# Transformer with a mixture of experts: expert inner activations computed feature-major, routing weights laid over partitions through DRAM

## The reference

```python
x = x + attn_part                                   # four layers
xf = layernorm(x).reshape(S, 128)                   # S = 8192 tokens
shared_out = silu(xf @ shared_gate_w.T) * (xf @ shared_up_w.T) @ shared_down_w.T   # 256 inner features
scores = sigmoid(xf @ router_w.T)                   # 16 experts; 4 groups of 4
# the best 2 groups by their two best biased scores, the best 4 experts in them, weights w normed to 1
g = einsum('sc,ech->esh', xf, gate_w); u = einsum('sc,ech->esh', xf, up_w)         # 32 inner features each
hw = silu(g) * u * combine.T[:, :, None]            # combine: w, or 0 where not chosen
x = x + shared_out + einsum('esh,ehc->sc', hw, down_w)
```

## Time and profile before

| what | value |
|---|---|
| median of 3 runs | 2311.6 us (2310.13 to 2312.68) |
| the profiled execution's own time | 2312.34 us |
| its span, first to last instruction | 2310.4 us |
| mean granted TensorE clock | 0.991 of full speed |
| busy over the span | PE 96%, PEld 82%, DVE 82%, ACT 80%, POOL 53% |
| block of experts | from about 1997 us to the end |
| 2080 to 2280 us: busy of 200 us | PE 200.0, PEld 160.8, DVE 152.3, ACT 118.2, POOL 75.0 |

### The profile page before, as it was taken

One profiled execution on the slowest core, in us unless ns is written; L12 is line 12 of the kernel. 1 busy time (PEld: TensorE's weight loads), 2 busy tenths in 40 slices (PEclk: granted clock), 3 DMA queues, 4 the chain that ended last, 5 costly groups with the idle time before them and its releaser, 6 DMA issues. The chain is left out here.

```text
span 2310.4 us, 81563 instructions
## 1 busy us (share of the span) xinstructions
PE 2206.6 (96%) x30592; PEld 1900.8 (82%) x30592; DVE 1894.9 (82%) x4687; ACT 1846.8 (80%) x2741; POOL 1233.4 (53%) x2217
## 2 busy tenths in 40 slices
PE   4899999999999999999999999999999999799998
PEld 3788888888888888888888888888888888688887
DVE  6788888888888888888888888888878886577774
ACT  3688888888888888888888888888878888656554
POOL 4555666655655555556555556565555554333332
PEclk8999999999999999999999999999999999999999
DMA  5444443433344343344434434433444342111100
GB/s 136 125 123 131 124 113 107 111 107 110 109 112 117 107 111 107 108 111 111 111 109 112 111 108 110 112 108 106 113 120 113 107 111 82 31 29 29 28 24 19
DMA packets 268388, 229.55 MB, mean 99 GB/s; under 512 B 37216, under 2 KB 266720, under 8 KB 268000
## 3 DMA queue, kind: packets, MB, share of 16 engines
q1 hardware_dynamic: 268000, 224.32, 35.2%
HBM read 14.46 MB, written 4.19 MB: 8 GB/s over the span
## 5 line engine op out<-in xcount | busy, mean ns | idle before, releaser
L985 DVE TENSOR_REDUCE rowmax<-bank 128x4 f32<-128x1024 f32 (+1 forms) x768 | 908.9, 1215 | 90.1 <-PE bank L582 87.7
L802 ACT ACTIVATE probs<-bank 128x1024 f32<-128x1024 f32 x768 | 737.6, 1024 | 124.0 <-PE bank L641 112.8
L641 PE MATMUL bank<-qstack,kstack 64*128 64x128 f32 (+1 forms) x4096 | 424.5, 300 | 14.7 <-DMA qstack<-maxrows 14.7
L582 PE MATMUL bank<-kstack,qstack 62*128 62x256 f32 (+1 forms) x4096 | 416.7, 301 | 6.5 <-DMA qstack<-base_turned 6.5
L641 PEld LDWEIGHTS bank<-qstack,kstack 64*128 64x128 f32 x4096 | 316.7, 192 | 17.2 <-DMA qstack<-maxrows 17.2
L582 PEld LDWEIGHTS bank<-kstack,qstack 62*128 62x128 f32 x4096 | 316.1, 193 | 6.9 <-issue 6.9
L1148 POOL CAST xn1T_parts<-xn1T 128x256 fp32r<-128x256 f32 x128 | 50.9, 397 | 460.1 <-ACT xn1T L810 460.1
L714 PE MATMUL bank<-w,hidden 128*128 128x128 f32 x2048 | 285.4, 283 | 3.3 <-ACT hidden L850 2.8
L604 PE MATMUL bank<-maskT_half,pick_half 64*128 64x128 bf16 (+1 forms) x3072 | 269.6, 241 | 15.2 <-ACT probs L802 5.4
L661 PE MATMUL bank<-probs,v_pad 128*32 128x256 f32 x4096 | 271.0, 382 | 0.6 <-DVE v_tok L966 0.6
L544 PE MATMUL bank<-mask_half,pick_half 64*128 64x128 bf16 (+1 forms) x3072 | 268.3, 242 | 2.1 <-DVE rowmax L985 0.9
(11 more groups left out here) (149 smaller groups left out, 5099.5 us busy)
## 6 DMA issues: line engine op xcount, KB each, us to landing
qstack<-base SPq DMA_DIRECT2D x384, 128.0 KB, 2.5
kstack<-base SPq DMA_DIRECT2D x384, 128.0 KB, 2.6
qstack<-base_turned SPq DMA_DIRECT2D x384, 128.0 KB, 2.4
turn_x<-turn_c SPq DMA_DIRECT2D x512, 32.0 KB, 1.8
ctx_den<-ctxT_raw SPq DMA_DIRECT2D x256, 64.0 KB, 2.0
ctx_num<-ctxT_raw SPq DMA_DIRECT2D x256, 64.0 KB, 2.0
qstack<-maxrows SPq DMA_DIRECT2D x256, 16.0 KB
out<-ot SPq DMA_DIRECT2D x16, 256.0 KB, 2.4
```

The costliest lines, as they stand in the source:

```text
L582: last = pe.matmul(bank[:, b0 + b, i * wide:(i + 1) * wide], qstack[rows, r, p0 + i, t * 128:(t + 1) * 128], kstack[rows, r, p0 + i, 0:wid ...
L641: last = pe.matmul(bank[:, b0 + b, i * wide:(i + 1) * wide], kstack[rows, r, p0 + i, kt * 128:(kt + 1) * 128], qstack[rows, r, p0 + i, q0: ...
L802: act.activation(probs[:, k], bank[:, A_BANK[k]:A_BANK[k] + 2, :], ACT.Exp, scale=SCALE).then_inc(exp_done[k], 1)
L985: dve.tensor_reduce(rowmax[:, n % 2, t, :, p0:p0 + heads], bank[:, M_BANK[k]:M_BANK[k] + 2, :].rearrange("p b (h c) -> p b h c", h=heads), ...
```

## The change

Only the block of experts is changed (and two constants are added, which moves its lines and those of the layers by two). The stationary operand is now a block of 128 inner features of the weights, and the four tiles of a group, 512 tokens, move past it: for each of FE = 6 feature blocks f one gate product and one up product of 512 columns (`product(q, f)`), whose result is [128 features x 512 tokens], one PSUM bank each. That is the layout the down product wants: `h_turn`, the copies to `hT` and their semaphores are gone, and `down` reads `hw` directly. ACT's silu and DVE's gating now run once per feature block (6 of 512 elements per partition, where 4 of 768 were).

The routing weight now has to vary over the partitions by expert and over the free axis by token. `combine` is transposed on TensorE (`combine_turn`, one matmul per group), copied out by ACT (`rows_out`), stored by SP as 16 rows of 512 numbers in DRAM (`rows_kept`), and read back by four DMAs, each of which repeats four of those rows on 32 partitions (`spread`), together 1 MB into the single buffer `factors`. POOL then multiplies four blocks of [128 x 512] in place (`weighted`), with a full second operand. The normalisation (`norm`) moves from DVE to POOL. The down product of a group runs one group later, two banks hold its results, and the store of a group is split in two DMAs.

```diff
+FE, FR = GU // 128, E * EH // 128
+DOWN_ORDER = tuple(range(FR, FE)) + tuple(range(FR))
...
-        combine = sb("combine", [128, 2, GT, E])
-        gate_act = sb("gate_act", [128, 2, GU])
-        act_all = sb("act_all", [128, 2, GU])
-        hw = sb("hw", [128, 2, E * EH])
-        hT = sb("hT", [128, GU // 128, 128])
+        combine = sb("combine", [128, E, GT])
+        rows = sb("rows", [E * GT, 2, 128])
+        factors = sb("factors", [128, FR, GT * 128])
+        gate_act = sb("gate_act", [128, 2, GT * 128])
+        hw = sb("hw", [128, 2, FE, GT * 128])
         ot = sb("ot", [128, 2, GT, D])
+        rows_kept = nc.dram_tensor("rows_kept", (2, E, GT * 128), F32, kind="Internal").ap()
...
+            def spread(q):
+
+                sp.wait_ge(rows_ready, q + 1)
+                at_least(sp, factors_landed, 16 * SPREAD * (q - 1))
+                sp.dma_start(rows_kept[q % 2].rearrange("e (t n) -> (e t) n", t=GT), rows[:, q % 2]
+                             ).then_inc(rows_stored, 16)
+                sp.wait_ge(rows_stored, 16 * (q + 1))
+                at_least(sp, hw_ready, FR * q)
+                for e in range(SPREAD):
+                    sp.dma_start(factors[e * EH:(e + 1) * EH],
+                                 rows_kept[q % 2].rearrange("(f e) n -> e f n", e=SPREAD)[e:e + 1]
+                                 .broadcast_to([EH, FR, GT * 128])).then_inc(factors_landed, 16)
...
+            for q in SLOTS:
                 if live(q):
+                    spread(q)
+                if live(q + 3):
+                    load(q + 3)
+                if live(q - 2):
+                    store(q - 2)
...
-            def product(n, v, u, i):
-
-                if i == 0:
-                    at_least(pe, act_ready, n - 1)
-                if n == 0 and i == 0:
+            def product(q, f):
+
+                n = FE * q + f
+                if n == 0:
                     pe.wait_ge(weights_split, 2)
-                if u == 0 and i == 0:
-                    pe.wait_ge(xT_low, n // GT + 1)
-                last = product_of_parts(pe, bank[:, 3 * (u % 2) + i, :],
-                                        [xT_parts[:, v % 2, p, u] for p in range(2)],
-                                        [w_in_parts[:, p, i * 512:(i + 1) * 512] for p in range(2)])
-                if i == 2:
-                    last.then_inc(in_done, 1)
-
-            def h_turn(n, u, half):
-
-                if half == 0:
-                    pe.wait_ge(hw_ready, n + 1)
-                    at_least(pe, hT_ready, 2 * n)
-                else:
-                    pe.wait_ge(hT_ready, 2 * n + 1)
-                for i in range(3):
-                    c = 3 * half + i
-                    src = hw[:, u % 2, c * 128:(c + 1) * 128] if c < E * EH // 128 else \
-                        act_all[:, u % 2, c * 128:(c + 1) * 128]
-                    last = pe.transpose(bank[:, 7, i * 128:(i + 1) * 128], src, eye[:])
-                last.then_inc(h_turned, 1)
-
-            def down(n):
-                pe.wait_ge(hT_ready, 2 * (n + 1))
+                if f == 0:
+                    pe.wait_ge(xT_low, q + 1)
+                x = [xT_parts[:, q % 2, p].rearrange("p t c -> p (t c)") for p in range(2)]
+                at_least(pe, gate_ready, n - GATE_BANKS + 1)
+                product_of_parts(pe, bank[:, GATE_BANK + n % GATE_BANKS, :],
+                                 [w_in_parts[:, p, f * 128:(f + 1) * 128] for p in range(2)], x).then_inc(gate_done, 1)
+                at_least(pe, act_ready, n - UP_BANKS + 1)
+                product_of_parts(pe, bank[:, UP_BANK + n % UP_BANKS, :],
+                                 [w_in_parts[:, p, GU + f * 128:GU + (f + 1) * 128] for p in range(2)], x
+                                 ).then_inc(in_done, 1)
+
+            def combine_turn(q):
+                pe.wait_ge(combine_ready, q + 1)
+                pe.wait_ge(xT_ready, min(q + 2, NG))
+                pe.wait_ge(score_ready, q + 1)
+                pe.transpose(bank[0:E * GT, TURN_BANK, 0:128], combine[:].rearrange("p e t -> p (e t)"),
+                             eye[:]).then_inc(combine_turned, 1)
+
+            def down(q, t):
+                n = GT * q + t
+                if t == 0:
+                    pe.wait_ge(act_ready, FE * (q + 1))
                 if n == 0:
                     pe.wait_ge(weights_landed, 16)
-                at_least(pe, out_ready, n)
-                pe.wait_ge(xT_ready, min((n + 2) // GT + 2, NG))
-                pe.wait_ge(score_ready, min((n + 1) // GT + 2, NG))
-                for c in range(GU // 128):
-                    last = pe.matmul(bank[:, 6, 0:D], hT[:, c], w_down[:, c], start=(c == 0),
-                                     stop=(c == GU // 128 - 1))
+                at_least(pe, out_ready, n - 1)
+                for i, c in enumerate(DOWN_ORDER):
+                    if t == 0 and c < FR:
+                        pe.wait_ge(hw_ready, FR * q + c + 1)
+                    last = pe.matmul(bank[:, OUT_BANK + n % OUT_BANKS, 0:D], hw[:, q % 2, c, t * 128:(t + 1) * 128],
+                                     w_down[:, c], start=(i == 0), stop=(i == FE - 1))
                 last.then_inc(down_done, 1)
...
+            for q in SLOTS:
+                if live(q + 1):
+                    x_turn(q + 1)
+                if live(q):
+                    product(q, 0)
+                if live(q):
+                    combine_turn(q)
+                if live(q - 1):
+                    down(q - 1, 0)
+                if live(q + 1):
+                    router(q + 1)
+                if live(q):
+                    product(q, 1)
+                if live(q):
+                    product(q, 2)
+                if live(q - 1):
+                    down(q - 1, 1)
+                if live(q):
+                    product(q, 3)
+                if live(q - 1):
+                    down(q - 1, 2)
+                if live(q):
+                    product(q, 4)
+                if live(q):
+                    product(q, 5)
+                if live(q - 1):
+                    down(q - 1, 3)
...
+            for q in SLOTS:
+                if live(q + 1):
+                    xT_out(q + 1)
+                if live(q):
+                    gate(q, 0)
+                if live(q):
+                    rows_out(q)
+                if live(q + 1):
+                    scores(q + 1)
+                for f in range(1, FE):
+                    if live(q):
+                        gate(q, f)
...
+            def gating(q, f):
+
+                n = FE * q + f
+                at_least(dve, down_done, GT * (q - 1))
                 dve.wait_ge(gate_ready, n + 1)
-                dve.tensor_tensor(act_all[:, u % 2], g[:, GU:2 * GU], gate_act[:, u % 2], ALU.mult
+                dve.wait_ge(in_done, n + 1)
+                dve.tensor_tensor(hw[:, q % 2, f], bank[:, UP_BANK + n % UP_BANKS, :], gate_act[:, n % 2], ALU.mult
                                   ).then_inc(act_ready, 1)
...
+            for q in SLOTS:
+                if live(q - 2):
+                    result(q - 2, 3)
+                if live(q + 2) and q + 2 > 1:
+                    residual(q + 2)
+                if live(q):
+                    gating(q, 0)
+                if live(q + 1):
+                    routing_groups_1(q + 1)
+                if live(q - 1):
+                    result(q - 1, 0)
+                if live(q):
+                    gating(q, 1)
+                if live(q):
+                    gating(q, 2)
+                if live(q + 1):
+                    routing_groups_2(q + 1)
+                if live(q - 1):
+                    result(q - 1, 1)
+                if live(q):
+                    gating(q, 3)
+                if live(q + 1):
+                    routing_experts(q + 1)
+                if live(q - 1):
+                    result(q - 1, 2)
+                if live(q):
+                    gating(q, 4)
+                if live(q + 1):
+                    weights_of_experts(q + 1)
+                if live(q):
+                    gating(q, 5)
...
+            def power(q):
+                pool.wait_ge(mv_ready, q + 1)
+                pool.tensor_scalar(ve[:], mv[:, :, 1], 1e-5, None, ALU.add).then_inc(ve_ready, 1)
+                pool.wait_ge(ve_ready, q + 1)
+                pool.tensor_tensor(rstd[:], ve[:], expo[:], ALU.pow).then_inc(rstd_ready, 1)
+
+            def norm(q):
+                pool.wait_ge(rstd_ready, q + 1)
+                pool.wait_ge(xn_turned, q)
+                for t in range(GT):
+                    last = pool.tensor_scalar(xn[:, t], h_groups[:, q, t], mv[:, t, 0:1], rstd[:, t:t + 1],
+                                              ALU.subtract, ALU.mult)
+                last.then_inc(xn_ready, 1)
+
+            def weighted(q, f):
+
+                pool.wait_ge(factors_landed, 16 * SPREAD * (q + 1))
+                pool.wait_ge(act_ready, FE * q + f + 1)
```

(12 more changed lines are left out.)

227 lines of the change are left out of this document (70 added, 157 removed).

## The result

The changed kernel takes **2269.8 us** (median of 4 runs, 2266.8 to 2274.6), the kernel before 2312.1 in the same comparison: a ratio of 0.982, 95% interval 0.9807 to 0.9832. The forecast was 2272.5 us, faster. The profiled execution spans 2268.3 us.

The account below looks back on a forecast made before the run. DVE, occupied 12.7 + 3.6 = 16.3 us per group, was taken to bound the expert block in lockstep with TensorE (floor 15.74). First group's last gating at 2020.0, 14 groups to 2248.2, span 2270.7, forecast 2272.5 us; range 2258 to 2301.

Parts of the forecast that it names:

- The last step of the sum: Whole kernel: from the forecast span of 2270.7 us to the forecast median of 2272.5, using profiled-run offsets 1.9 and 0.7.
- The first step: TensorE per group of the expert block: 18.64 - 2.16 (transposes) - 0.86 (products) + 0.12 (combine transpose) = 15.74 us.
- rival B: Expert block: TensorE alone bounds the group at 15.74 us, POOL waits falling in DVE's free time; 2264 us, chance 0.20.
- And it decides: Expert block: DVE's occupied 16.3 us sets the group, in lockstep with TensorE, which waits 0.5 us in each group.
- The waits for POOL: DVE in each expert group: operations held until POOL's instructions end, 3.6 us for 1.6 before; ends 0 and 7.8.
- The path of the weights: Expert block: factors land 9.2 us behind the transpose of combine (store 2.4, loads 6), covered by some 2 us.
- Rival E: Expert block: single-buffered repeated load holds the group; at 22.4 us load, 27.9 per group and 2435 us; chance 0.09.
- my break-even: Expert block: the repeated load decides from 19.1 us per group, a load of 13.6 us or 77 GB/s.
- My rule for it: Expert block: with one factors buffer, a group takes load + 5.1 (multiplies) + 0.4 us.
- The end: Last group: 13.0 us rest of slot, 5.5 for four down products, 0.4 result, then 3.6 from last store's issue.
- Rival D: Expert block: TensorE's waits halve its clock for 3 us per group, costing 1.5 more: 17.8, 2294 us; chance 0.06.

Follow-up runs that it names:

- d3: Changed kernel with POOL multiplying only 16 of the 512 columns of each of the four pieces (output differs); 2260.5 us, ratio 0.9773.
- t1: Kernel before the change with one transpose instead of three in each half of the turning of h (output differs); 2283.9 us, ratio 0.9878.
- d1: Changed kernel with two of the six chunks of each down product issued twice, lengthening TensorE's stream (output wrong); 2293.6 us, ratio 0.9927.
- d2: Changed kernel with the normalisation moved back from POOL to VectorE, ahead of the routing of experts in each slot; 2322.6 us, ratio 1.003.
- s3: Changed kernel with SyncE's load of x and store of the finished group moved ahead of the rows and factors in each slot; 2265.1 us, ratio 0.9785.
- e1: Changed kernel with the four repeated loads of a group issued twice, the second time after the first have landed; 2341.1 us, ratio 1.0136.
- b1: Changed kernel with product 1 and the router moved ahead of the first down product in each slot; 2267.0 us, ratio 0.9790.

## Why the prediction was right, and where it was not

The time was forecast within 3 us, but by luck: from two large errors of opposite sign, of which the one at the start hung on when the clock came back in this execution. The last step of the sum has a slip too: 2270.7 + 1.9 - 0.7 is 2271.9, not 2272.5. Against the forecast's own dates, in the profiled execution:

| | forecast | measured | difference |
|---|---|---|---|
| last gating of group 0 ends | 2020.0 | 2026.4 | +6.4 |
| 14 groups more | 228.2 (16.3 each) | 218.3 (15.6 each) | -9.9 |
| from there to the last store's issue | 18.9 | 21.3 | +2.4 |
| to the end of the span | 3.6 | 2.3 | -1.3 |

**TensorE's removed work: right.** The first step gave a floor of 15.74 us; d3 reaches 15.19. The products came to 8.74 of the forecast 8.78, the transpose of combine to 0.11 of 0.12. Missing were 0.32 us in four down products and 0.14 in router and x_turn. t1 shows why for the down products: a wait hidden in their length. Of the other 0.14 no run tells the cause. The floor was 0.55 us too high, for rival B as well.

**VectorE in lockstep with TensorE, "And it decides": the wait came, its size was wrong.** The waits for POOL were sized at 3.6 us. By forms they are 2.5 (residual 0.60, `wsel` 0.80, `combine` 0.54, `chosen` 0.26, `crep` 0.28 over d3's means); VectorE's busy time shows 2.1, 14.1 for d3's 12.0. By the forecast's own measure, the group less VectorE's waits for TensorE and ScalarE (0.6 us of 15.49, and 2.5 of 15.19 in d3), VectorE is occupied for 14.9 us where 16.3 were forecast, and for 12.7 in d3, just the 12.7 forecast without the waits. So the waits alone were mis-sized, by some 1.4 us, and with them the group. With TensorE's floor at 15.19 the two engines nearly balance. TensorE is the bound for its 15.19 us, as d1 and d3 show from both sides, and the steady group was nearest to rival B, which I gave 0.20. But it was not "no wait at all": the 3.7 us that the twelve groups have above 15.187 each are 2.7 of waits for VectorE's last gating, at eight first down products, and 1.0 of late multiplies. That is the wait that I forecast, at the place that I forecast, at 0.2 us per group for 0.5. d2, which adds VectorE's norm, comes near the forecast in its undisturbed groups, 16.1 us.

**The normalisation on POOL: mis-sized beyond its bounds.** Taken at 1.4 us, ends 1.1 and 2.4; measured 3.13 to 3.16. My upper end came from two-operand work of the same size. No run shows that it cost anything in the steady state. At the start it made the 4.82 us wait: the forecast kept product 0 "at 2001.3 as before", although the new order puts `x_turn(1)`, and with it norm(1), ahead of it. But that wait is not what made the +6.4. The block began 0.7 us later; from the first turning of x to the last gating of group 0 the forecast has 22.9 us, the changed kernel 28.6, and s3, with a wait of 4.65 us at the same place, 23.8. So 0.9 us are left where the clock came back at 2010 us, and 4.8 us are its standing at 0.50 until 2017. The earlier trace rows had shown the low clock and I charged nothing for it. What makes it come back early or late, with the same instructions ahead, no run tells. The first of the 14 groups paid again, 18.2 us, behind TensorE's wait of 2.61 us for `combine` and a clock of 0.59 from 2028 to 2036 us; the other thirteen take 15.4 each.

**The multiplies: right**, 1.25 to 1.31 us each against 1.28; the Trainium skill's figure (GPSIMD Engine Reference, "Elementwise — side-by-side cycle accounting"), by which I had estimated 1.11, was too low here, and the row of a like instruction was the better guide.

**The path of the weights: right in kind.** Landed 7.2 us behind the first issue (9.1 once) for 6; the small store 1.8 for 2.4. Rival E's ring was the right one, and e1 puts numbers on it: at a load of 14.3 us the kernel takes 2341, where my break-even was 2312 at 13.6. My rule for it, load + 5.1 + 0.4, gives 19.8 at 14.3; measured 19.8 in that round.

**The end**: the rest of the last slot took 13.2 us for 13.0. The last four down products took 7.7 for 5.5, because the first of them waited 2.3 us for the last two multiplies, which end at about 2259.8 and 2261.1; the forecast had them covered. From the last store's issue to the end it is 2.3 us for 3.6; the store is half as large now, but no run takes the split away.

**Rival D** did not happen in the changed kernel's steady state, but at its start and in d2 it did, and d2 shows that its price was too low: with waits of 1.4 to 1.8 us its groups took some 4.5 us more than its undisturbed ones, of which 3.15 are the clock's, for the 1.5 of my rival, and the rest the longer wait.

## What to carry to other kernels

Where removed work lies on the engine that is never idle, count it from starts to starts and expect all of it, but look whether the lengths of its neighbours hide a wait that goes too. When work moves from one engine to another, ask of the receiving engine at the first turn of the loop, where nothing is ahead of it: there the same 3 us that are free later stand on the path, and the clock may be charged on top. An engine that fits under the bound by less than 1 us with its waits is one edit away from being the bound, and then the cost can be not that edit's time alone but the clock's too.

## What was not expected of the hardware

- A POOL tensor_scalar with two per-partition operands on 128 x 128 numbers takes 0.79 us, four of them 3.1, where one two-operand POOL instruction on 128 x 512, as many numbers, takes 1.25 to 1.31. VectorE does the four in 1.11.
- In d2, waits of TensorE of 1.41 and 1.82 us are followed by a granted clock of 0.50, and a wait of 0.43 (2121.23 us) is not. The length of the wait alone does not decide it: in b1 a wait of 1.40 (2141.85 us) left the clock at 1.00, and two waits of 0.73 at the end were followed by 0.58 in b1 and by 1.00 in the changed kernel.
- Four loads of 256 KB, each repeating four rows of DRAM on 32 partitions, land 7.2 us behind the first issue with others beside them; twice that in series took 14.3.
